# A two-block AdaLN transformer on one core: the late half of the expert weights moves from a stage of its own into the experts' first two units

## The reference

```python
t = x.reshape(-1, D)                                  # 4096 tokens
logits = t @ Wg.T + bg                                # 8 experts
probs = jax.nn.softmax(logits, axis=-1)
topw, topi = jax.lax.top_k(probs, 2)
topw = topw / jnp.sum(topw, axis=-1, keepdims=True)
combine = jnp.sum(jax.nn.one_hot(topi, E) * topw[..., None], axis=1)
# for every expert e, over all tokens:
gate, up = jnp.split(t @ w1[e].T, 2, axis=-1)
acc = acc + combine[:, e][:, None] * ((silu(gate) * up) @ w2[e].T)
```

## Time and profile before

| | us |
|---|---|
| median of 3 runs (841.31, 843.66, 843.99) | 843.66 |
| the profiled execution | 841.44 |
| its span, first to last instruction | 839.5 |
| TensorE busy in it | 718.9 |
| VectorE busy in it | 626.9 |

### The profile page before, as it was taken

The page is one execution under the profiler, slowest core; times in us unless marked ns, Lnnn a source line. Parts: engine busy times, 40 slices in busy tenths (PEclk is TensorE's granted clock), DMA queues, the critical chain, the costliest instruction groups (busy, mean ns, idle before and its releaser), DMA issues. The chain is left out here.

```text
span 839.5 us, 17146 instructions
## 1 busy us (share of the span) xinstructions
PE 718.9 (86%) x5737; PEld 504.7 (60%) x5737; DVE 626.9 (75%) x1426; ACT 539.5 (64%) x1195; POOL 386.1 (46%) x482
## 2 busy tenths in 40 slices
PE   5668899989998857899999997499998939999996
PEld 3323333333333336888999997377776638877874
DVE  3658988978988736778777763478889848888884
ACT  3126676767776735788788885388887716555563
POOL 6234455445442010421220000789998627676764
PEclk9999999999999977999999999799999969999997
DMA  3765655554453003000000000000000532544530
GB/s 91 101 122 82 93 73 70 69 70 68 73 73 37 4 17 127 1 1 1 2 1 1 2 1 1 2 2 2 2 2 2 132 77 75 140 113 126 141 85 25
DMA packets 76423, 44.18 MB, mean 53 GB/s; under 512 B 6144, under 2 KB 74160, under 8 KB 76208
## 3 DMA queue, kind: packets, MB, share of 16 engines
q1 hardware_dynamic: 76336, 43.07, 27.0%
HBM read 27.83 MB, written 2.25 MB: 36 GB/s over the span
## 5 line engine op out<-in xcount | busy, mean ns | idle before, releaser
L593 DVE TENSOR_REDUCE att_negmax<-att_p_max 128x2 f32<-128x512 f32 x256 | 170.4, 688 | 35.0 <-PE att_p_max L473 32.7
L694 ACT ACTIVATE att_probs<-att_p_sT 128x1024 f32<-128x1024 f32 x128 | 130.8, 1025 | 60.5 <-PE att_p_sT L479 58.1
L473 PE MATMUL att_p_max<-att0p_QK 48*128 48x256 bf16 x512 | 102.6, 291 | 29.2 <-DVE att_negmax L593 16.0
L2098 POOL TENSOR_TENSOR moe_z_lo<-moe_z,moe_z_hi 128x512 fp32r<-128x512 f32 x64 | 96.7, 1523 | 55.1 <-ACT moe_z_hi L2051 54.4
L479 PE MATMUL att_p_sT<-att0p_QK 51*128 51x256 bf16 x512 | 99.4, 279 | 0.6 <-ACT att_probs L694 0.3
L473 PEld LDWEIGHTS att_p_max<-att0p_QK 48*128 48x128 bf16 x512 | 29.0, 96 | 110.1 <-DVE att_negmax L593 54.9
L989 POOL TENSOR_TENSOR ffn0s_rstd<-ffn0s_var_eps,top_minus_half 128x2 f32<-128x2 f32 x16 | 11.6, 722 | 180.4 <-DVE ffn0s_var_eps L976 180.4
L943 PE MATMUL ffn0s_p_h<-ffn0s_u_hi,top_ffn_all 128*128 128x256 f32 x256 | 71.0, 310 | 16.9 <-DVE ffn0s_u_lo L1204 16.5
L501 PE MATMUL att_p_o<-att_probs,att0p_V 128*32 128x256 f32 x1024 | 83.2, 398 | 0.5 <-ACT att_probs L694 0.5
L1204 DVE TENSOR_TENSOR ffn0s_g_lo<-ffn0s_g,ffn0s_g_hi 128x512 fp32r<-128x512 f32 x64 | 48.6, 776 | 42.3 <-ACT ffn0s_g_hi L1148 41.1
L2089 DVE TENSOR_TENSOR moe_z<-moe_act_u,top_ffn_all 128x512 f32<-128x512 f32 x64 | 73.0, 1141 | 2.2
(11 more groups left out here) (248 smaller groups left out, 1945.4 us busy)
## 6 DMA issues: line engine op xcount, KB each, us to landing
top_ffn_all<-combine SPq DMA_DIRECT2D x32, 512.0 KB, 6.5
att0p_QK<-att_parts SPq DMA_DIRECT2D x192, 64.0 KB
att_raw<-in_L_ffn_h_w SPq DMA_DIRECT2D x8, 256.0 KB, 4.1
out_x<-top_X SPq DMA_DIRECT2D x8, 256.0 KB, 2.3
top_X<-in_x SPq DMA_DIRECT2D x2, 768.0 KB, 9.7
top_wo_all<-gates SPq DMA_DIRECT2D x4, 256.0 KB, 4.4
top_gbo_all<-gates SPq DMA_DIRECT2D x4, 256.0 KB, 5.0
top_wo_all<-gates SPq DMA_DIRECT2D x1, 1024.0 KB, 7.1
```

The lines of the kernel that those rows point to most:

```text
L473: mm = pe.matmul(bank(at)[:, i, :], QK[r][rows, g, 0, i * P:(i + 1) * P], QK[r][rows, g, 1, :], start=True, stop=True)
L593: dve.tensor_reduce(negmax[:, :, w, g], bank(at)[:], AX.X, ALU.max, negate=True).then_inc(drained, 1)
L694: act.activation(probs[g % 2][:, t % 2], p_sT[t % 2][:], ACT.Exp).then_inc(exped, 1)
L2098: pool.tensor_tensor(z_lo[e % RING][:], z[e % RING][:], z_hi[e % RING][:].bitcast(F32), ALU.subtract).then_inc(z_lo_ready, 1)
```

## The change

The stage `router` goes. The recipe is cut into its single steps, and for the late 16 tiles they are spread: maximum, subtraction and exponential at the end of attention 1; one expert's comparisons after each z of unit 0; the rank sum after the first z of unit 1, pick, total and reciprocal with share after its third, fourth and fifth; the transpose at the end of TensorE's unit 1, into a PSUM tile of its own; ScalarE's copy in unit 2 ahead of its second silu; and the store on SP in its round of unit 1, after the loads for unit 3 and ahead of the store of X.

```diff
@@ attention1 @@
+        late_gating = gating_steps(k, sem, EARLY * NT, TILES_ALL, "late_gating")
 ...
             for n in range(FIRST, LAST):
                 act_step(act, n)
+            late_gating.act_exp(act)
 ...
             for n in range(FIRST, LAST):
                 dve_step(dve, n)
+            dve.wait_ge(logits_ready, B)
+            late_gating.dve_top(dve)
@@ gating_steps: the same instructions, in functions that can be called apart @@
+    def dve_top(dve):
         then(dve, dve.tensor_reduce(top, logits, AX.X, ALU.max))
         dve.tensor_tensor(shifted, logits, top.unsqueeze(2).to_broadcast(shape), ALU.subtract
                           ).then_inc(g.shifted_ready, 1)
+    def dve_beats(dve, e):
+        for lo, hi, op in ((0, e, ALU.is_ge), (e + 1, E, ALU.is_gt)):
+            if hi > lo:
+                ins = dve.tensor_tensor(k.beats[:, tiles, e, lo:hi], logits[:, :, lo:hi],
+                                        logits[:, :, e:e + 1].to_broadcast([P, t1 - t0, hi - lo]), op)
+        return ins
+    def dve_rank_sum(dve):
+        then(dve, dve.tensor_reduce(rank, k.beats[:, tiles], AX.X, ALU.add))
+    def dve_pick(dve):
         then(dve, dve.scalar_tensor_tensor(out=weight, in0=rank, scalar=TOP - 0.5, in1=weight,
                                            op0=ALU.is_lt, op1=ALU.mult))
+    def dve_total(dve):
+        then(dve, dve.tensor_reduce(k.total[:, tiles], weight, AX.X, ALU.add))
+    def dve_share(dve):
+        then(dve, dve.reciprocal(k.rtotal[:, tiles], k.total[:, tiles]))
+        dve.tensor_tensor(weight, weight, k.rtotal[:, tiles].unsqueeze(2).to_broadcast(shape), ALU.mult).then_inc(g.combined, 1)
-def router(nc, k, wsb):
 ...
@@ experts @@
+        p_c = ps("p_c", [P, P])
+        gating = gating_steps(k, sem, EARLY * NT, TILES_ALL)
 ...
+        def pe_turn_combine(pe):
+            pe.wait_ge(gating.combined, 1)
+            pe.transpose(p_c[:], k.weight[:, CT_TILES:].rearrange("p t e -> p (t e)"), k.ident[:]).then_inc(comb_turned, 1)
@@ pe_unit, last in the loop over e @@
+                if u == 1 and e == E - 1:
+                    pe_turn_combine(pe)
 ...
+        def act_combine(act):
+            act.wait_ge(comb_turned, 1)
+            act.activation(k.cT[:, 1, :], p_c[:], ACT.Copy).then_inc(comb_ready, 1)
@@ act_unit, first in the loop over e @@
+                if u == 2 and e == 1:
+                    act_combine(act)
@@ dve_unit, last in the loop over e @@
                 if e == LAG + 2 and not first:
                     dve_add(dve, u - 1)
+                if u == 0:
+                    ins = gating.dve_beats(dve, e)
+                    if e == E - 1:
+                        gating.then(dve, ins)
+                if u == 1 and e == 0:
+                    gating.dve_rank_sum(dve)
+                if u == 1 and e == 2:
+                    gating.dve_pick(dve)
+                if u == 1 and e == 3:
+                    gating.dve_total(dve)
+                if u == 1 and e == 4:
+                    gating.dve_share(dve)
@@ SP, in its round of unit u @@
+                if u == 1:
+                    sp.wait_ge(comb_ready, 1)
+                    store_combine(sp, k, 1)
+                    sp.wait_ge(k.c_stored, 32)
                 sp.wait_ge(x_added, u + 1)
@@ build @@
         attention1(nc, k)
-        router(nc, k, wsb)
         experts(nc, k, out)
```

More of the change, by code:

```diff
@@ L1897, in gating_tensors, with gating_steps @@
             for n in range(2)]
-def gating_steps(k, sem, t0, t1):
+def gating_steps(k, sem, t0, t1, tag="gating"):
     g = Names()
[L1903 to L1906, removed]
+    g.chain = sem(tag + "_chain")
+    g.shifted_ready = sem(tag + "_shifted_ready")
+    g.weight_ready = sem(tag + "_weight_ready")
+    g.combined = sem(tag + "_combined")
     g.count = 0
@@ L1916, in then @@
         dve.wait_ge(g.chain, g.count)
-    def dve_rank(dve):
+    def dve_top(dve):
         then(dve, dve.tensor_reduce(top, logits, AX.X, ALU.max))
@@ L1922, in dve_rank @@
                           ).then_inc(g.shifted_ready, 1)
+    def dve_beats(dve, e):
[6 more added lines that the diff above has]
+        then(dve, dve.tensor_reduce(rank, k.beats[:, tiles], AX.X, ALU.add))
+    def dve_rank(dve):
+        dve_top(dve)
         for e in range(E):
[L1925 to L1928, removed]
+            ins = dve_beats(dve, e)
         then(dve, ins)
-        then(dve, dve.tensor_reduce(rank, k.beats[:, tiles], AX.X, ALU.add))
+        dve_rank_sum(dve)
     def act_exp(act):
@@ L1934, in act_exp @@
         act.activation(weight, shifted, ACT.Exp).then_inc(g.weight_ready, 1)
-    def dve_weigh(dve):
-        total, rtotal = k.total[:, tiles], k.rtotal[:, tiles]
-        dve.wait_ge(g.weight_ready, 1)
+    def dve_pick(dve):
         then(dve, dve.scalar_tensor_tensor(out=weight, in0=rank, scalar=TOP - 0.5, in1=weight,
                                            op0=ALU.is_lt, op1=ALU.mult))
-        then(dve, dve.tensor_reduce(total, weight, AX.X, ALU.add))
-        then(dve, dve.reciprocal(rtotal, total))
-        dve.tensor_tensor(weight, weight, rtotal.unsqueeze(2).to_broadcast(shape), ALU.mult).then_inc(g.combined, 1)
@@ L1946, in gating_steps @@
-    g.dve_rank, g.act_exp, g.dve_weigh = dve_rank, act_exp, dve_weigh
-    return g
-def router(nc, k, wsb):
[L1952 to L1980, removed]
+    def dve_total(dve):
+        then(dve, dve.tensor_reduce(k.total[:, tiles], weight, AX.X, ALU.add))
@@ new lines, in dve_share, with dve_weigh @@
+    def dve_share(dve):
+        then(dve, dve.reciprocal(k.rtotal[:, tiles], k.total[:, tiles]))
+        dve.tensor_tensor(weight, weight, k.rtotal[:, tiles].unsqueeze(2).to_broadcast(shape), ALU.mult).then_inc(g.combined, 1)
+    def dve_weigh(dve):
+        dve.wait_ge(g.weight_ready, 1)
+        dve_pick(dve)
+        dve_total(dve)
+        dve_share(dve)
+    g.then, g.dve_top, g.dve_beats, g.dve_rank_sum, g.dve_rank = then, dve_top, dve_beats, dve_rank_sum, dve_rank
+    g.act_exp, g.dve_pick, g.dve_total, g.dve_share, g.dve_weigh = act_exp, dve_pick, dve_total, dve_share, dve_weigh
@@ L1998, in experts @@
         p_m = ps("p_m", [P, U])
+        p_c = ps("p_c", [P, P])
+        gating = gating_steps(k, sem, EARLY * NT, TILES_ALL)
+        comb_turned = sem("comb_turned")
+        comb_ready = sem("comb_ready")
         gate_made = sem("gate_made")
```

## The result

Over 20 runs of each kernel the median went from 849.06 to 843.35 us. The ratio is 0.9949, with a 95% interval of 0.9924 to 0.9973: the change makes the kernel faster by 0.5%, about 4.3 us (2.3 to 6.5). Ratios and intervals here leave out the executions that fell in a slower state, so they are not the ratios of the medians. The profiled execution of the new kernel took 842.60 us, with a span of 840.5. That is longer than the profiled execution of before (841.44), so two whole spans cannot be compared; their stages can.

The account below looks back on a forecast made before the run. TensorE in the experts was taken as the bound, with the hole before them worth its full length. Cost 5.4 less gain 7.3 gave −1.9 us; from base 842.6 the forecast was 840.7 us, range 835.8 to 844.0.

Parts of the forecast that it names:

- The hole: Between attention 1's last logits and the first expert matmul: that matmul moves from 689.14 to 681.8, 7.3 us gained.
- The lost rounds: Experts' unit 0: comparisons make VectorE's z lose to GpSimd's z_lo, so a round takes 2.58 us, 0.50 above TensorE's 2.08.
- the gate of (1,3): Gate matmul of unit 1, expert 3: waits for the product behind the rank sum, 4.13 us late.
- Unit 1: Experts' second unit: rank sum, pick, total and share delay z; unit 2's first gate matmul starts 4.9 us late.
- The wait of the down matmul of (1,6) for its z_lo: Unit 1, expert 6: z_lo lasts until 731.82, so its down matmul starts at 731.88 instead of 726.57, 5.3 late.
- the term of 5.4: Total cost in us of the steps added to the experts' units 0 and 1, as TensorE's delay.
- The level: Whole-kernel base: mean 842.6 us of four known times (841.31, 841.44, 843.66, 843.99), from which the 1.9 us gain was taken.
- flow: Time from the first expert matmul to unit 3's first gate matmul, 51.29 us before; the experts' added cost was forecast as 5.4.
- full hiding: Rival, experts: all additions hide in VectorE's idle time, giving 835.3 us; all or most hidden had chance 0.20.
- The clock: Rival, units 0 and 1: the clock drops while TensorE waits, costing 1.7 us, giving 842.4; chance 0.10.
- The lost rounds ended with unit 1: Against the rival that lost rounds continue past unit 1, 4 us per further unit, 848.7 with two; chance 0.06.

Follow-up runs that it names:

- the third experiment: The kernel before, router stage kept, plus two small unread maxima over logits after every z of unit 0; time from first expert matmul to unit 3's first gate 54.76 us.
- The second comparison: Kernel before, new kernel and the sixth experiment's kernel timed side by side: medians 847.13, 843.76 and 838.69 us; new against before ratio 0.996.
- the fifth and sixth kernel: New kernel with comparisons and rank sum ahead of unit 0, four short steps together; sixth also moves maximum, subtraction, exponential there. Flow 50.61 and 51.16 us; sixth's ratio 0.9885.
- the fourth kernel: The kernel before plus one unread two-element VectorE instruction after every z of unit 0; first expert matmul to unit 3's first gate matmul 51.62 us.

## Why the prediction was right or wrong

**The hole: right.** 7.3 us were summed, 7.34 measured, and with it each part: 0.04 to the maximum, 0.96 to the end of the exponential, 1.05 for the boundary (1.04 summed).

**The lost rounds: right.** They last 2.58 us, z takes 1.69, and the delay of VectorE by 0.25 alone causes them, as the third experiment shows. The Trainium skill's rule on the port that both share ("SBUF — State Buffer", "Who interferes with whom") agrees with z at 0.69 us alone and 1.69 behind z_lo. In unit 0 the step was right to a tenth: the gate of (1,3) was to be 4.13 us late and was 4.06.

**Unit 1: the size nearly right, a step wrong.** The first gate of unit 2 was to be 4.9 late by the product of (1,6), and was 725.60 − 686.65 − 33.96 = 4.99 late. That this number fits is luck: it had been as late since the down matmul of (1,0) (716.05), and by another wait: that matmul needs the PSUM bank that ScalarE empties into yT, and on ScalarE this stands behind z_hi of (1,1), which waits for the z behind the rank sum. ScalarE in the new kernel:

```profile
714.54 0.63 ACT L2049 ACTIVATE moe_z_hi<-moe_z 128x512 fp32r<-128x512 f32 x1 [1.46 <-DVE moe_z L2093]
715.08 0.82 ACT L2055 ACTIVATE moe_yT<-moe_p_y,top_mod 128x256 f32<-128x256 f32 x2
```

I had named what waits on TensorE for the rank sum, not what is queued behind z_hi on ScalarE. The wait of the down matmul of (1,6) for its z_lo, 0.4 us in the sum, did not come: TensorE was late enough already. So the term of 5.4 measured 4.9 up to unit 3 (second profile 4.7), and the transpose did not lie in a wait, as I had said, but cost at most 0.1. That TensorE never waits inside a unit was read off unit 1 of before, which takes 17.07 us; units 3 to 6 take 17.33 to 17.37 there, so something holds them up a little. They take as long in the new kernel, so this cost the forecast nothing.

**The level: wrong, and the change too small.** The step that failed is the last one of the sum, the base. I took the mean of four executions of before (841.3 to 844.0), 842.6, as its time and set the range around it. Twenty runs reach from 841.3 to 857.8 with a median of 849.06, 6.5 us above that base; the three runs known then are the three shortest of the twenty. On that median the measured ratio means 844.7, beyond the range's top of 844.0. The change was summed too small as well: 1.9 us, where the first comparison measured 4.3 (2.3 to 6.5); hole and flow account for 0.5 of this difference, the term of 5.4 that measured 4.9. The second comparison, 3.4 (0.4 to 6.3), does not exclude 1.9. The new kernel's median, 843.35, is inside the range only because the two errors go opposite ways, and that is luck. So is the ratio of the forecast to the median then known, 840.7 / 843.66 = 0.9965, inside the measured interval: 1.1 of its 3.0 us is the step from that median to the mean, not a gain that was summed.

Profiles of the same code show how far the level can move. The first instruction of the dense feed-forward in the profile of before and in that of the doubled rank sum, and the busy time by stretch of attention 0 in both:

```profile
306.97 0.49 DVE L969 BATCH_NORM_STATS2 ffn0s_stats<-top_X 128x6 f32<-128x128 f32 x2 [1.21 <-PEq L110]
25.00:307.00 282.00, 240.61 (x2385) 93.61 (x2385) 225.24 (x456) 177.91 (x247) 107.28 (x123) 0.99 0.48 68
```

```profile
317.70 0.48 DVE L969 BATCH_NORM_STATS2 ffn0s_stats<-top_X 128x6 f32<-128x128 f32 x2 [1.21 <-PEq L110]
25.00:317.00 292.00, 252.05 (x2385) 96.62 (x2385) 224.70 (x454) 178.39 (x247) 107.44 (x123) 0.94 0.46 66
```

The same instructions take 10.7 us more, with a mean granted clock of 0.94 instead of 0.99. The profile of before has the earliest end of attention 0 among the eleven profiles of this case; the second profile of the new kernel has it at 315.74 us. The clock goes with the whole time as well: the executions of the new kernel under 841 us had a mean granted clock of 0.958 to 0.962, those over 850 us one of 0.941 to 0.949. Why the three first executions of before were all short is not shown. One execution is no base to a quarter of a percent, and here three were none either.

**What stays open.** By hole and flow the change is worth 2.45 us in the first profile of the new kernel and 2.7 in the second (7.35 less 4.68). Counted to the end of the span, with the clock that fell there sooner or later, it is 3.8 and 2.9. The two comparisons say 4.3 (2.3 to 6.5) and 3.4 (0.4 to 6.3) us, and all of these lie inside both intervals. Whether another 1 or 2 us come from somewhere, the runs do not tell. How soon the clock rises in the experts is hardly it: 4.8 and 2.9 us after the first matmul in the two profiles of the new kernel (4.9 in that of before), and their flows differ by 0.2.

The rivals: full hiding was wrong for this placement (4.9 us were paid) and right for another (the fifth and sixth kernel). The clock stayed at 1.00 from 704 to 738 us, through the longest waits. The lost rounds ended with unit 1: from unit 3 on, z alternates as before.

## What to carry to other kernels

Idle time by sum does not tell where small work can go: where two engines shut each other out for whole instructions, as VectorE's z and GpSimd's z_lo do here, a margin of a tenth of a microsecond decides the order, and a short instruction in every round can flip it in every round. Look at one round for who asks first and by how much; then put such work in one piece, where the engine waits for something else anyway (here the start of the stage), rather than in many small ones. And to predict within a percent, compare stages of the trace, since the level of whole executions may move by more than the change.

## What the runs showed of the hardware

A VectorE instruction of two elements with one SBUF input took 1.26 us where GpSimd's z_lo was running, and 0.15 where it was not (the fourth kernel); I had expected only instructions with two SBUF inputs to wait. (The Trainium skill, "SBUF — State Buffer", section "Who interferes with whom", allows it for a `tensor_scalar` in a mode that uses both ports; no other run here shows it.) And the time to the end of attention 0 differs by 10.7 us between two executions of the same code, with the granted clock at 0.99 in one and 0.94 in the other; at the end of the span the last seven matmuls with ScalarE's scaling and the add took 4.42 us at 0.50 and 3.27 at 1.00.
